# An adaptive layer norm, attention and mixture-of-experts block: the second layer norm in batches of four tiles, other load and queue orders

## What is computed

```
mod = silu(c) @ wmod                       # c 1x256, wmod 256x1536: sa, ca, ga, sb, cb, gb
ga, gb = sign(.) * max(|.|, 0.25)
h = layernorm(x) * (1 + ca) + sa           # x 1024x256
x = x + ga * attn(h)                       # attn: a second layer norm (gamma, beta), one causal head,
                                           #   key size 256, o_proj, plus its own residual h
h = layernorm(x) * (1 + cb) + sb
x = x + gb * (moe(h) + shared(h))          # 32 experts, top 4 in 2 of 4 groups, 64 slots each; all float32
```

## Time and profile before

| what | value |
|---|---|
| median of 3 runs | 176.83 us (175.35 to 176.85) |
| the profiled execution | 175.42 us |
| its span in the trace | 173.7 us |
| TensorE busy | 147.5 us (85%) |
| VectorE busy | 108.9 us (63%) |
| ScalarE busy | 62.4 us (36%) |
| GpSimd busy | 55.4 us (32%) |
| TensorE / VectorE on the chain that ended last | 50% / 32% |

### The profile page before, as it was taken

The page is one execution under the profiler, slowest core; times in us unless marked ns, Lnnn a source line. Parts: engine busy times, 40 slices in busy tenths (PEclk is TensorE's granted clock), DMA queues, the critical chain, the costliest instruction groups (busy, mean ns, idle before and its releaser), DMA issues.

```text
span 173.7 us, 2811 instructions
## 1 busy us (share of the span) xinstructions
PE 147.5 (85%) x938; PEld 102.1 (59%) x938; DVE 108.9 (63%) x386; ACT 62.4 (36%) x167; POOL 55.4 (32%) x77
## 2 busy tenths in 40 slices
PE   0198769999999899997598969996999989879993
PEld 0153534887547767685274624886666656568882
DVE  2679964836955688799884598382566664321563
ACT  3257578633055526375243623012333333200000
...
GB/s 130 340 321 405 423 400 357 348 349 347 349 348 348 348 136 70 0 0 38 30 4 0 44 60 4 68 123 115 36 37 101 94 73 69 50 46 298 411 319 181
DMA packets 21808, 31.34 MB, mean 180 GB/s; under 512 B 2032, under 2 KB 17942, under 8 KB 21794
## 3 DMA queue, kind: packets, MB, share of 16 engines
...
...
## 4 chain that ended last, share of the span: by engine, by line
PE 50%; DVE 32%; ACT 7%; issue 5%; DMA 3%; SPq 1%; DVEq 0%; ACTq 0%
PE bank L1054 16%; PE bank L1351 10%; PE bank L1397 6%; PE bank L1391 4%; DMA w_sb<-in_L_wmod_dram 3%; PE bank L1370 3%; DVE bmax L797 3%; DVE st L708 2%; DVE rows L818 2%; PE bank L1184 2%; PE bank L1361 2%; DVE base L811 2%; PE bank L1328 2%; PE bank L1158 2%; PE bank L1162 2%
## 5 line engine op out<-in xcount | busy, mean ns | idle before, releaser
L444 POOL DMA_INDIRECT arena<-token_rows,gather_idx x16 | 16.4, 1025 | 67.2 <-DVE gather_idx L907 62.6
L1351 PE MATMUL bank<-w_sb,arena 128*64 128x128 f32 x256 | 17.3, 278 | 3.4 <-ACT arena L655 1.3
L1351 PEld LDWEIGHTS bank<-w_sb,arena 128*64 128x64 f32 x256 | 13.9, 136 | 7.7 <-issue 4.1
L453 POOL DMA_INDIRECT results<-aT,res_idx x14 | 14.0, 999 | 11.0 <-DVE aT L997 7.9
L1184 PE MATMUL bank<-arena 128*128 128x256 f32 x72 | 17.2, 382 | 0.3 <-issue 0.3
L1184 PEld LDWEIGHTS bank<-arena 128*128 128x128 f32 x72 | 13.1, 190 | 2.5 <-issue 0.9
L1054 PE MATMUL bank<-w_sb,h2T 128*128 128x512 f32 x12 | 7.6, 769 | 8.2 <-DMA w_sb<-in_L_wmod_dram 8.2
L1017 DVE TENSOR_TENSOR h2T<-h2T,bank 128x256 f32<-128x256 f32 x8 | 3.4, 421 | 15.7 <-ACT h2T L672 15.7
L537 ACT ACTIVATE prob<-bank,nmax 128x512 f32<-128x512 f32 (+3 forms) x12 | 6.9, 581 | 12.4 <-DVE nmax L801 12.4
L1397 PE MATMUL bank<-w_sb,ident 128*128 128x256 f32 x48 | 10.6, 382 | 0.0
L556 ACT ACTIVATE h2T<-bank,modc 128x128 f32<-128x128 f32 x16 | 6.4, 455 | 11.5 <-PE bank L1192 11.5
...
## 6 DMA issues: line engine op xcount, KB each, us to landing
w_sb<-in_L_ffn_w_dram SPq DMA_DIRECT2D x12, 1024.0 KB, 12.3
...
```

Source lines behind the costliest of these rows:

```text
L444: nc.gpsimd.indirect_dma_start(out=slot_in[:, r, :], out_offset=None, in_=rows_d, in_offset=bass.IndirectOffsetOnAxis(ap=gather_idx[:, r:r ...
L453: nc.gpsimd.indirect_dma_start(out=results_d, out_offset=bass.IndirectOffsetOnAxis(ap=res_idx[:, r:r + 1], axis=0), in_=ob[:, g % 4, (r % ...
L1351: last = t.matmul(bank[4 + g % 2][CAP * side:CAP * side + CAP, o:o + F], slotT[:, k, CAP * e:CAP * e + CAP], w[:, e, k, :], start=(k == 0) ...
```

## The change

- x is loaded whole ahead of the first third of `wmod`.
- TensorE runs 45 bf16 products of 128x128 into bank 0, whose results nobody reads, ahead of `mod_rows(0)`; they wait for the bf16 identity.
- `shift(1)` stands ahead of `mod01_evac` on VectorE.
- The second norm's moments are taken for four tiles at once. VectorE scales and shifts the even tiles, GpSimd the odd ones. `hn_tile` runs on ScalarE for even tiles and on VectorE for odd ones.
- The transposes of the pair of tiles 2 and 3 go to bank 0 instead of the ring, and VectorE empties them (`xn1_evac`).
- `fold_qk` goes ahead of `mod_rows(1)`; `mod_rows(2)` behind `project_q(0)`; `turn_h(2)` and `turn_h(3)` behind `project_v(1)`.
- `gates` is split: ga ahead of `q_evac(0)`, gb behind `mod_columns`, which itself goes behind `row_max(1)`.

The core of the diff (semaphore names and renumbered calls are left out):

```diff
-            plan = ["wT0", "wT1", "wT2", "hn0", "hn1", "gateT", "hn2", "hn3"]
+            plan = ["wT0", "wT1", "wT2", "hn0", "gateT", "hn2", "hn3"]
...
-        RSQRT = [(0, 0, 4), (0, 4, 4)] + [(1, 2 * j, 2) for j in range(NB)] + [(2, i, 1) for i in range(NT)]
+        RSQRT = [(0, 0, 4), (0, 4, 4)] + [(1, 0, 4), (1, 4, 4)] + [(2, i, 1) for i in range(NT)]
         MOMENTS = (mv1, mv2, mv3)
 
-        scaled_by_pool = lambda i: sum(1 for tile in range(i + 1) if tile % 4)
+        WARM = 45
         pos_bank = lambda b: bank[7 if b else 0]
...
                 sp.dma_start(xin[:, 2 * j:2 * j + 2, :], x_d[:, 2 * j:2 * j + 2, :]).then_inc(x_loaded[j], 16)
-                if j == 1:
-                    sp.dma_start(wmod_a, wmod_d[:, :, 0:512]).then_inc(wmod_loaded[0], 16)
+            sp.dma_start(wmod_a, wmod_d[:, :, 0:512]).then_inc(wmod_loaded[0], 16)
...
-            for i in range(NT):
-                if i % 4 == 0:
-                    continue
+            for i in range(1, NT, 2):
                 pool.wait_ge(xhat_done, i + 1)
                 g.tensor_tensor(h[:, i, :], h[:, i, :], mod[:, 1, :], ALU.mult).then_inc(xhat_scaled, 1)
-                if i % 2:
-                    pool.wait_ge(xhat_scaled, scaled_by_pool(i))
-                    g.tensor_tensor(h[:, i, :], h[:, i, :], mod[:, 0, :], ALU.add).then_inc(h_pool, 1)
+                pool.wait_ge(xhat_scaled, i // 2 + 1)
+                g.tensor_tensor(h[:, i, :], h[:, i, :], mod[:, 0, :], ALU.add).then_inc(h_pool, 1)
 
             pool.wait_ge(gagb_done, 1)
...
             pool.wait_ge(shared_loaded, 48)
+            pool.wait_ge(gagb_done, 2)
...
                 xhat_tile(i)
             rsqrt_seed(1)
             wT_evac(0)
-            for i in range(4, NT):
-                xhat_tile(i)
             wT_evac(1)
             wT_evac(2)
+            for i in range(4, 7):
+                xhat_tile(i)
             rsqrt_seed(2)
             act.wait_ge(wqk_mm, 1)
             a.copy(wqk, bank[3][:, :].rearrange("p (k n) -> p k n", k=KT)).then_inc(wqk_done, 1)
-            rsqrt_seed(3)
-            for i in range(4):
-                hn_tile(i)
+            xhat_tile(7)
+            hn_tile(0)
+            hn_tile(2)
             act.wait_ge(small_loaded, 64)
             xn_evac(0)
-            xn_evac(1)
-            rsqrt_seed(4)
-            rsqrt_seed(5)
             mod_evac(0)
-            hn_tile(4)
-            hn_tile(5)
+            rsqrt_seed(3)
+            q_evac(0)
             mod_evac(1)
-            q_evac(0)
             act.wait_ge(ring_filled, ring["gateT"] + 1)
             a.copy(gateT[:, :, :], ring_bank("gateT")[:, 0:KT * E].rearrange("p (k e) -> p k e", k=KT))\
              .then_inc(ring_drained, 1)
+            hn_tile(4)
             hn_tile(6)
-            hn_tile(7)
             xn_evac(2)
             xn_evac(3)
             exp_tile(0)
...
+                if which == 1:
+                    tiles = list(tiles[0::2]) + list(tiles[1::2])
                 for i in tiles:
+                    if which == 1 and i % 2:
+                        dve.wait_ge(h_pool, i // 2 + 1)
...
-            def make_h(j):
-
-                if j % 2 == 0:
-                    dve.wait_ge(xhat_done, 2 * j + 1)
-                    chain(v.tensor_tensor(h[:, 2 * j, :], h[:, 2 * j, :], mod[:, 1, :], ALU.mult))
-                else:
-                    dve.wait_ge(xhat_scaled, scaled_by_pool(2 * j))
-                v.tensor_tensor(h[:, 2 * j, :], h[:, 2 * j, :], mod[:, 0, :], ALU.add).then_inc(h_dve, 1)
-                dve.wait_ge(h_dve, j + 1)
-                dve.wait_ge(h_pool, j + 1)
-                moments(2 + j, h)
+            def make_h(first):
+
+                pair = (first, first + 2)
+                for i in pair:
+                    dve.wait_ge(xhat_done, i + 1)
+                    step(v.tensor_tensor(h[:, i, :], h[:, i, :], mod[:, 1, :], ALU.mult))
+                settle()
+                for i in pair:
+                    v.tensor_tensor(h[:, i, :], h[:, i, :], mod[:, 0, :], ALU.add).then_inc(h_dve, 1)
+                dve.wait_ge(h_dve, first // 2 + 2)
+
+            def hn_tile(i):
+
+                dve.wait_ge(hstat_done, i // 4 + 1)
+                v.tensor_scalar(hn[:, i, :].rearrange("q (k p) -> q p k", k=KT),
+                                h[:, i, :].rearrange("q (p k) -> q p k", k=KT), rstd[:, 1, i:i + 1],
+                                nmr[:, 1, i:i + 1], ALU.mult, ALU.add).then_inc(hn_dve, 1)
+
+            def xn1_evac():
+
+                dve.wait_ge(small_loaded, 64)
+                dve.wait_ge(hn1_mm, 1)
+                for k in range(KT):
+                    last = v.tensor_scalar(xnT[:, k, 256:512], bank[0][:, 256 * k:256 * k + 256],
+                                           gb_col[:, 0, k:k + 1], gb_col[:, 1, k:k + 1], ALU.mult, ALU.add)
+                last.then_inc(hn1_done, 1)
 
...
-            def gates():
-
-                dve.wait_ge(mod_raw, 2)
-                both = mod[:, 2:6:3, :]
-                chain(v.scalar_tensor_tensor(out=gabs[:, :, :], in0=both, scalar=-1.0, in1=both,
+            def gates(n):
+
+                dve.wait_ge(mod_raw, n + 1)
+                gate = mod[:, 2 + 3 * n, :]
+                chain(v.scalar_tensor_tensor(out=gabs[:, n, :], in0=gate, scalar=-1.0, in1=gate,
                                              op0=ALU.mult, op1=ALU.max))
-                step(v.tensor_scalar(gabs[:, :, :], gabs[:, :, :], 0.25, None, ALU.max))
-                chain(v.tensor_scalar(both, both, 0.0, 2.0, ALU.is_ge, ALU.mult))
-                v.scalar_tensor_tensor(out=both, in0=both, scalar=1.0, in1=gabs[:, :, :],
+                step(v.tensor_scalar(gabs[:, n, :], gabs[:, n, :], 0.25, None, ALU.max))
+                chain(v.tensor_scalar(gate, gate, 0.0, 2.0, ALU.is_ge, ALU.mult))
+                v.scalar_tensor_tensor(out=gate, in0=gate, scalar=1.0, in1=gabs[:, n, :],
                                        op0=ALU.subtract, op1=ALU.mult).then_inc(gagb_done, 1)
-                dve.wait_ge(gagb_done, 1)
+                dve.wait_ge(gagb_done, n + 1)
 
...
             x_moments(0)
             shift(0, xstat_done)
             x_moments(1)
+            shift(1, xstat_done)
             mod01_evac()
-            shift(1, xstat_done)
             make_h(0)
-            make_h(1)
+            moments(2, h)
             shift(2, hstat_done)
+            hn_tile(1)
+            hn_tile(3)
+            make_h(4)
+            xn1_evac()
+            moments(3, h)
+            gates(0)
+            q_evac(0)
+            wvo_evac()
             shift(3, hstat_done)
-            make_h(2)
-            make_h(3)
-            shift(4, hstat_done)
-            shift(5, hstat_done)
-            q_evac(0)
-            gates()
-            wvo_evac()
-            mod_columns()
+            hn_tile(5)
+            hn_tile(7)
             row_max(0)
             row_max(1)
+            mod_columns()
+            gates(1)
             for j in range(2):
                 vo_evac(j)
             dve.wait_ge(consts, 15)
...
+            pe.wait_ge(consts, 5)
+            for _ in range(WARM):
+                t.matmul(bank[0][:, 0:P], ident_bf[:, :], ones_bf[:, :], start=True, stop=True)
             pe.wait_ge(silu_c_done, 1)
             pe.wait_ge(wmod_loaded[0], 16)
             mod_rows(0)
 
-            pe.wait_ge(consts, 3)
...
             def turn_h(j):
-                pe.wait_ge(hn_done, 2 * j + 2)
-                b = ring_open(f"hn{j}")
+                pe.wait_ge(hn_act, j + 1)
+                pe.wait_ge(hn_dve, j + 1)
+                if j == 1:
+                    pe.wait_ge(mod01, 1)
+                b = bank[0] if j == 1 else ring_open(f"hn{j}")
                 for i in range(2):
                     for k in range(KT):
                         last = t.transpose(b[:, 256 * k + P * i:256 * k + P * i + P], hn[:, 2 * j + i, P * k:P * k + P],
                                            ident[:, :])
-                last.then_inc(ring_filled, 1)
+                last.then_inc(hn1_mm if j == 1 else ring_filled, 1)
 
             def project_q(half):
-                pe.wait_ge(ring_drained, ring[f"hn{2 * half + 1}"] + 1)
+                if half:
+                    pe.wait_ge(ring_drained, ring["hn3"] + 1)
+                else:
+                    pe.wait_ge(ring_drained, ring["hn0"] + 1)
+                    pe.wait_ge(hn1_done, 1)
                 pe.wait_ge(wqk_done, 1)
                 if half:
                     pe.wait_ge(qT_act, 1)
...
 
             def project_v(j):
-                pe.wait_ge(ring_drained, ring[f"hn{j}"] + 1)
+                if j != 1:
+                    pe.wait_ge(ring_drained, ring[f"hn{j}"] + 1)
                 pe.wait_ge(wvo_done, 1)
                 if j % 2:
                     pe.wait_ge(modc_done, 1)
...
+            fold_qk()
             pe.wait_ge(wmod_loaded[1], 16)
             mod_rows(1)
-            fold_qk()
```

(7 more changed lines are left out.)

17 lines of the change are left out of this document (10 added, 7 removed).

## The result

The changed kernel takes **181.6 us** (median of 4 runs, 180.6 to 184.6) where the kernel before takes 176.6 beside it: ratio **1.028**, 95% interval 1.020 to 1.036. It is slower, outside the predicted range of 174.7 to 179.3. Ratios and intervals here leave out executions more than 1.5% above the fastest of their kernel; where the medians of all executions give a ratio that is 0.4% or more away, it stands behind as "all". The profiled execution took 181.97 us, its span is 180.2, against 175.42 and 173.7.

What follows compares the result with a forecast made beforehand. The prediction took the end to follow `project_q(0)`'s start and TensorE's unbroken run to `turn_p(0)`. `turn_p(0)` moving from 37.25 to 37.8, +0.5 us on 176.83, gave 177.3 us; own range 176.2 to 178.6, with rivals 174.7 to 179.3.

Steps and rivals of the forecast that it cites:

- Part 1, loads: At the start: matrix lands 1.1 us later, x some 2.5 us earlier, `shift(1)` ends at about 11.4.
- Part 2, warm-up: Ahead of `mod_rows(0)`: warm-up free, over at 8.7; `mod_rows(0)` takes 1.9 us from 9.0, `mod01` at 12.25 against 12.44.
- (b): Warm-up ahead of `mod_rows(0)` is in the way: `mod01` 3.2 us later, 180.5 us in all; chance 0.08.
- (d): Warm-up does not warm, a pause drops the clock: `mod_rows(0)` ends at 12.75, +1.35, 178.7 us; chance 0.06.
- Part 3, second norm: Second layer norm of tiles 0 to 3: `hstat` at 18.35, `project_q(0)` starts at 22.65 instead of 26.04.
- Part 4: From `project_q(0)` to `turn_p(0)`: TensorE would arrive at 35.6, 1.65 us early, but waits; `turn_p(0)` at 37.8 against 37.25.
- the wait for `exp_tile(0)`: Ahead of `turn_p(0)`: TensorE stands 1.95 us while ScalarE finishes two evacuations and the exponential, at 37.55.
- `project_v(1)` waits 0.25 for `mod_columns`: Ahead of `project_v(1)`: VectorE ends `mod_columns` at 32.9, TensorE is ready at 32.65, adding 0.25 us.
- "The same distance from `turn_p(0)` to the end": Behind `turn_p(0)`: TensorE is full, so a shift of `turn_p(0)` reaches the end whole, +0.5 us.
- rival (a): Faster, no VectorE-GpSimd locks: `turn_p(0)` at 36.5, later gains reach the end, -2.05 us, 174.8 us; chance 0.13.
- `gates(1)` "free": Behind `mod_columns` on VectorE: `gates(1)` costs nothing, since its readers stand far behind.
- Rival (c): Slower, VectorE-GpSimd locks dear: `turn_p(0)` at 39.0 to 39.5, 178.6 to 179.1 us; chance 0.13.

Runs made afterwards that it cites:

- experiment 4: The changed kernel without the 45 warm-up products: ratio 1.028 to the kernel before.
- experiment 8: The changed kernel again, unaltered, on another chip: ratio 1.032 to the kernel before.
- experiment 1: The changed kernel with `mod_rows(2)` moved back ahead of `project_q(0)`: ratio 1.022 to the kernel before.
- experiment 7: The kernel before with the 45 warm-up products and nothing else: ratio 1.005 to the kernel before.
- experiment 2: The changed kernel with 30 unread bf16 products of 128x128 ahead of `project_q(0)`: ratio 1.005 to the kernel before (all 1.013).
- experiment 9: The kernel before with only `mod_rows(2)` moved behind `project_q(0)`: ratio 1.019, 179.4 us against 176.2.
- experiment 3: The changed kernel with `turn_h(2)` and `turn_h(3)` ahead of `project_v(0)`: ratio 1.012 to the kernel before.
- experiment 14: The changed kernel with 24 unread products behind the first shared product and nothing else: ratio 1.013 to the kernel before.
- experiment 5: The changed kernel with 30 unread products ahead of `project_q(0)`, and `turn_h(2)` and `turn_h(3)` ahead of `project_v(0)`: ratio 1.001 to the kernel before.
- experiment 12: The kernel before with 24 unread products behind the first shared product: ratio 0.999 to the kernel before.
- experiment 13: The changed kernel, unread products ahead of `project_q(0)` (30) and behind the first shared product (24), `turn_h(2)`, `turn_h(3)` ahead of `project_v(0)`, `gates(1)` late: ratio 0.989.
- experiment 15: The same kernel as experiment 13, unaltered, on another chip: ratio 0.995 to the kernel before (all 0.991).
- experiment 16: The changed kernel, `mod_rows(2)` ahead of `project_q(0)`, `turn_h` early, `gates(1)` late, unread products ahead of `turn_h(2)` (12) and behind the first shared product (24): ratio 0.994.
- experiment 10: The changed kernel, 30 unread products ahead of `project_q(0)`, `turn_h(2)`, `turn_h(3)` ahead of `project_v(0)`, `gates(1)` behind two value evacuations: ratio 0.999 (all 1.006).

## Why the prediction was wrong

The forecast was 177.3 us, +0.5; measured are +5.0. By its own steps:

- **Part 1, loads: right.** `shift(1)` over at 11.44, forecast 11.4.
- **Part 2, warm-up: right.** 45 products in 4.73 us are 0.105 each, taken as 0.11; over at 8.45 (8.7); `mod_rows(0)` 1.96 us (1.9); `mod01` at 12.10 (12.25). The matrix did not hold it up: `mod_rows(0)` followed the warm-up at once at 8.41, forecast 9.0. Rivals (b) and (d), the warm-up too long or without effect, fall: without it, in experiment 4, `mod01` starts 1.4 us later than in experiment 8 (13.21 against 11.82) and `turn_p(0)` 1.7 (42.24 against 40.56), though the medians can't tell the two apart. Rival (d) did happen now and then, though: of 14 traces with the warm-up 12 have `mod_rows(0)` at 1.95 to 1.98 us, but in experiment 1 it took 3.75, behind an idle 0.68 us, and in experiment 7 2.39.
- **Part 3, second norm: right.** `hstat` at 18.38, where its last operation ends (forecast 18.35), `project_q(0)` 22.74 (forecast 22.65). VectorE's four products and sums took 1.29 + 1.71 = 3.0 us beside GpSimd, where I had 2.5. By the Trainium skill (SBUF — State Buffer, "Who interferes with whom") a VectorE operation with two SBUF inputs contends with a GpSimd operation that reads SBUF. This trace agrees: four of 0.41, the shorter duration in the earlier trace rows, would be 1.64.
- **Part 4: here the failure lies**, in one sum: "TensorE would arrive at 22.65 + 12.93 = 35.6". The 12.93 are durations of the kernel before at full clock. The prediction itself had written down that `project_q(0)` would begin about 2 us behind the last transposes (20.55 and 22.65), and that `mod_rows(2)` no longer stood there, and never asked what TensorE's clock does in such a hole, though in part 2 it had read the two levels of that clock from the earlier trace rows. `project_q(0)` ran at the lower level: 2.84 us more. 37.8 + 2.84 = 40.6; the trace has 40.57. That the two meet so closely is partly luck: the forecast's 0.25 for `mod_columns` did not come, and 0.2 of small terms that it did not have stand in its place. Experiments 1 and 2 (the gap filled: 3.67 us) and 9 (the move alone: 6.62) show it.
- **Part 4, the wait for `exp_tile(0)`: right to 0.01 us** (1.95 forecast, 1.94 measured), and experiment 3 takes it away and nothing else ahead of `turn_p(0)`. The wait could have cost more than itself: the clock stayed up behind it in the changed kernel (both traces) and experiment 4, and fell in experiments 1, 2 and 14 (39 to 44 us). What decides that is open.
- **Part 4, `project_v(1)` waits 0.25 for `mod_columns`: hidden** behind the slow `project_q(0)`; it came back as 0.52 us in experiment 1.
- **"The same distance from `turn_p(0)` to the end": wrong in this run.** To the fifth row maximum it is 16.46 against 16.40, so the loop is indeed TensorE's and rival (a), a gain passing on, has no ground. But by the last `norm_x2` another 1.62 us are lost to the second fall, at an idle stretch of 2.02 us that both kernels have. Why it falls there in most traces of the changed order (not in experiments 1, 3 and 5) and, by their mean clock, in perhaps four of ten runs of the kernel before is not settled; it is shown only that the five traces with the stretch filled (12 to 16) have no fall there, where seven of thirteen without have one.
- **`gates(1)` "free": not quite**, once the rest was mended: 3.07 us of VectorE beside GpSimd's residuals delayed the values by 0.46 (experiment 5), and behind two of the evacuations they held up the third, by 0.40 (experiment 10).
- The own range's lower end, 176.2, should be 176.1 by its own terms (176.83 - 0.75); nothing hangs on it.
- Rival (c), locks dear, gave 178.6 to 179.1 by another mechanism; the locks cost 0.5 us more than forecast at one place and were made up for at others.

Of the 6.5 us between the profiled executions 3.3 are explained at `turn_p(0)` (0.5 of them forecast, 2.84 the first fall) and 1.6 by the second fall; the 1.56 of the last stretch stay open. The medians lie only 5.0 apart, since the one of the changed kernel is 0.4 below its profiled execution and the one of the kernel before 1.2 above its own, which had a mean clock of 1.00.
